# Two transformer-like layers on one core: the shift rows of the second layer's attention as wide products with a mask, the last gate products in four banks, and a new order list

## The reference

```python
Q, K = apply_rope(Q), apply_rope(K)                      # 16 heads of 16
attn = einsum('bqhd,bkhd->bhqk', Q, K) * head_dim ** -0.5
attn = softmax(where(causal, attn, NEG_INF))
out = einsum('bhqk,bkhd->bqhd', attn, V) @ w_proj + b_proj
...
h = silu(tlin(x, w1_w, w1_s)) * tlin(x, w2_w, w2_s)      # 256 -> 1024, the gate products
h = gelu(tlin(h, h1_w, h1_s)); h = gelu(tlin(h, h2_w, h2_s))   # 1024 -> 1024
return tlin(h, w3_w, w3_s)                               # 1024 -> 256
```

## Time and profile before

| what | value |
|---|---|
| median of 3 runs | 1990.87 us (1989.52 to 1991.04) |
| time of the profiled execution | 1990.24 us |
| its span | 1988.5 us |
| PE busy | 1866.2 us, 94% |
| DVE busy | 1359.8 us, 68% |
| ACT busy | 904.1 us, 45% |
| POOL busy | 509.0 us, 26% |
| chain that ended last | PE 74%, DVE 14%, ACT 5%, issue 3% |

### The profile page before, as it was taken

The page is one execution under the profiler, slowest core; times in us unless marked ns, Lnnn a source line. Parts: engine busy times, 40 slices in busy tenths (PEclk is TensorE's granted clock), DMA queues, the critical chain, the costliest instruction groups (busy, mean ns, idle before and its releaser), DMA issues.

```text
span 1988.5 us, 40531 instructions
## 1 busy us (share of the span) xinstructions
PE 1866.2 (94%) x16217; PEld 1308.3 (66%) x16217; DVE 1359.8 (68%) x2382; ACT 904.1 (45%) x1134; POOL 509.0 (26%) x597
## 2 busy tenths in 40 slices
PE   7999999998999997787999999999999999999988
PEld 4665756565656664444677776776776776776767
DVE  5667686767677568778678678587587687686353
ACT  2556555645565654332434524524424434433411
POOL 2435343434444343111211203103103103112020
PEclk8899999999999999898999999999999999999999
DMA  7221212222322000400122231231231321321321
GB/s 191 54 53 43 60 34 62 50 58 50 82 51 63 2 23 1 170 1 16 46 83 73 65 88 48 76 95 30 75 96 33 94 86 51 87 71 57 114 67 43
DMA packets 171818, 126.36 MB, mean 64 GB/s; under 512 B 113944, under 2 KB 148720, under 8 KB 171248
## 3 DMA queue, kind: packets, MB, share of 16 engines
q1 hardware_dynamic: 170800, 123.74, 22.4%
q10 hardware_dynamic: 832, 0.01, 0.0%
HBM read 103.66 MB, written 20.03 MB: 62 GB/s over the span
## 4 chain that ended last, share of the span: by engine, by line
PE 74%; DVE 14%; ACT 5%; issue 3%; SPq 1%; POOL 1%; DMA 1%; DVEq 0%; ACTq 0%; POOLq 0%
PE ps L2028 24%; PE ps L2012 4%; PE ps L1077 4%; PE ps L1908 3%; PE ps L1971 3%; PE ps L982 3%; PE ps L2042 3%; PE ps L1937 3%; DVE b_maxima L1688 3%; PE ps L1951 2%; PE ps L1107 2%; PE ps L1955 2%; PE ps L1040 2%; PE ps L1022 2%; PE ps L1129 2%
## 5 line engine op out<-in xcount | busy, mean ns | idle before, releaser
L2028 PE MATMUL ps<-b_acts,b_hidden_w 128*128 128x512 f32 x2048 | 504.4, 399 | 0.7 <-DVEq L1769 0.7
L2028 PEld LDWEIGHTS ps<-b_acts,b_hidden_w 128*128 128x128 f32 x2048 | 376.3, 188 | 92.1 <-issue 12.9
L452 POOL TENSOR_SCALAR_AFFINE_SELECT a_probs<-a_probs 128x512 f32<-128x512 f32 (+1 forms) x224 | 166.1, 757 | 374.0 <-ACT a_probs L862 249.5
L1607 POOL TENSOR_SCALAR_AFFINE_SELECT b_work<-b_work 128x512 f32<-128x512 f32 x128 | 82.4, 657 | 659.6 <-ACT b_work L1833 659.5
L862 ACT ACTIVATE a_probs<-ps 128x2048 f32<-128x2048 f32 (+1 forms) x96 | 153.1, 1595 | 141.6 <-DVEq L712 104.8
L1865 ACT ACTIVATE b_acts_exact<-ps,c_s 128x512 f32<-128x512 f32 x128 | 88.2, 689 | 273.6 <-PE ps L2028 273.3
L1833 ACT ACTIVATE b_work<-ps 128x2048 f32<-128x2048 f32 (+1 forms) x96 | 153.3, 1596 | 88.5 <-PE ps L1955 87.0
L1688 DVE TENSOR_REDUCE b_maxima<-ps 128x4 f32<-128x2048 f32 (+3 forms) x128 | 187.8, 1488 | 3.3
L1778 DVE CAST b_acts<-b_acts_exact 128x512 fp32r<-128x512 f32 x128 | 60.5, 473 | 166.0 <-ACT b_acts_exact L1865 165.7
L1077 PE MATMUL ps<-a_probs,c_va 128*17 128x192 f32 (+4 forms) x2048 | 134.3, 380 | 4.7 <-issue 2.2
L1685 DVE TENSOR_TENSOR ps<-ps,c_causalr 128x512 f32<-128x512 f32 x128 | 86.1, 695 | 43.3 <-PE ps L1937 41.6
(11 more groups left out here) (242 smaller groups left out, 3611.5 us busy)
## 6 DMA issues: line engine op xcount, KB each, us to landing
b_hidden_w<-turned_h SPq DMA_DIRECT2D x128, 512.0 KB, 3.5
a_raw_next<-in_L_ffn_h_w SPq DMA_DIRECT2D x512, 16.0 KB, 1.8
turned_h<-a_staged SPq DMA_DIRECT2D x32, 256.0 KB, 2.1
a_x<-in_L_attn_x SPq DMA_DIRECT2D x8, 512.0 KB, 4.2
x_mid<-a_x SPq DMA_DIRECT2D x16, 256.0 KB, 2.2
c_x<-x_mid SPq DMA_DIRECT2D x8, 512.0 KB, 4.8
out<-c_x SPq DMA_DIRECT2D x16, 256.0 KB, 2.2
turned_w<-a_staged SPq DMA_DIRECT2D x12, 256.0 KB, 2.6
```

What stands on the lines that cost most here:

```text
L452: return nc.gpsimd.affine_select(out=z, in_=z, compare_op=ALU.is_ge, fill=0.0, base=0, pattern=[[0, blocks_n], [1, cols]], channel_multipl ...
L2028: ins = nc.tensor.matmul(here, view(hidden_w[:, m, k]), view(src[:, k, i]), start=(k + i == 0), stop=(k == NHID - 1 and i == 1))
```

## The change

1. `shift_cols` is a tile of its own, and `again` is one product of 512 columns: `shift_cols` as the stationary side, the identity four times over as the moving side. DVE multiplies it by `shift_rows`, so that each of the four 128-column blocks keeps the rows of its own query tile only. ACT's copy is gone.
2. `att` adds the shift with one set of four products for each key block, of 512, 384, 256 and 128 columns, with a stationary side of ones.
3. POOL's clearing of `shift_cols` no longer waits for the end of the first layer's attention.
4. In the last pass the gate products of odd hidden tiles go to banks 0 and 1, those of even ones to 6 and 7, and the rounding copy is made by ACT instead of DVE.
5. The order list is another one throughout. It has the same entries. The second layer's first entry is now at 711, and most entries have moved by a few places.

```diff
-        self.shift_rows = sb("shift_rows", [P, NT], F32R)
+        self.shift_rows = sb("shift_rows", [P, NT + 1], F32R)
...
+        once(nc.vector.memset(shift_rows[:, NT:NT + 1].bitcast(F32), 1.0))
...
-        return ("f0", "f1")[step[3]]
+        last_pass_odd = step[1] == B - 1 and step[2] % 2
+        return (("g0", "g1") if last_pass_odd else ("f0", "f1"))[step[3]]
...
-    shift = sb("shift", [P, P], F32R)
+    shift = kept.ksplit[:, 3]
+    shift_cols = sb("shift_cols", [P, 4, R])
...
-                first_filled(pool, "lin", QUADS * B - 1, 2)
-                first_filled(pool, "win", QUADS * B - 1, 1)
-                nc.gpsimd.memset(shift_cols, 0.0).then_inc(shift_zero, 1)
+                nc.gpsimd.memset(shift_cols[:], 0.0).then_inc(shift_zero, 1)
...
+            elif name == "again":
+                free = arrive(step)
+                by_tile = room[slot_of(step)].rearrange("p (t q) -> p t q", q=P)
+                nc.vector.tensor_tensor(shift.rearrange("p (t q) -> p t q", q=P), by_tile, shift_rows[:, 0:NT].bitcast(F32).unsqueeze(2).broadcast_to([P, NT, P]),
+                                        ALU.mult).then_inc(free, 1)
...
-                    nc.vector.tensor_copy(act_a[:, i, 0], z).then_inc(a_high, 1)
+                    if b < B - 1:
+                        nc.vector.tensor_copy(act_a[:, i, 0], z).then_inc(a_high, 1)
+                    else:
+                        dve.sem_inc(z_ready, 1)
...
+        def copy_high(i):
+            act.wait_ge(z_ready, i + 1)
+            nc.scalar.copy(act_a[:, i, 0], exact_a[:, i]).then_inc(a_high, 1)
...
-                nc.scalar.copy(shift[:], here[:, 0:P]).then_inc(free, 1)
...
+                if b == B - 1 and i:
+                    copy_high(i - 1)
+            elif step == ("up", B - 1, NHID - 1, 1):
+                copy_high(NHID - 1)
...
-                ins = nc.tensor.transpose(here[:, 0:P], shift_cols.rearrange("p h r -> p (h r)"), ident)
+                ins = nc.tensor.matmul(here.rearrange("p (t q) -> p t q", q=P), shift_cols[:].bitcast(F32R).rearrange("p h r -> p (h r)"),
+                                       identr[:, None, :].broadcast_to([P, NT, P]), start=True, stop=True)
...
-                    for t in range(kb, NT):
-                        at = o + (t - kb) * P
-                        for i in range(4):
-                            nc.tensor.matmul(here[:, i, at:at + P], shift_rows[rows_of(i), t:t + 1].broadcast_to([R, P]), shift[rows_of(i)],
-                                             start=True, stop=False, skip_group_check=True)
+                    for i in range(4):
+                        nc.tensor.matmul(here[:, i, o:o + S - kb * P], shift_rows[rows_of(i), NT:NT + 1].broadcast_to([R, P]), shift[rows_of(i), kb * P:S],
+                                         start=True, stop=False, skip_group_check=True)
```

More of the change, by code:

```diff
@@ L1206 @@
[L1206 to L1209, removed]
@@ new lines @@
+1:proj.1.2 1:proj.1.3 0:r.7.0 0:kk.7.1 1:ga.0 1:tq.1.0 1:out.0.0 1:tk.1.0 1:max.1.0.0 1:tq.1.1 1:max.1.0.1 1:out.0.1 1:tk.1.1 1:max.1.0.2 0:r.7.1
+0:last.7.0 1:xT.0 1:again.1.0 0:last.7.1 1:att.1.0.0 1:split.0 1:max.1.1.0 1:up.0.0.0 1:up.0.0.1 1:values.1.0.0 1:att.1.0.1 1:up.0.1.0 1:up.0.1.1
+1:att.1.0.2 1:max.1.1.1 1:tk.1.2 1:values.1.0.1 1:tq.1.2 1:max.1.1.2 1:up.0.2.0 1:again.1.1 1:max.1.2.0 1:values.1.0.2 1:up.0.2.1 1:up.0.3.0
+1:heads.1.0 1:att.1.1.0 1:up.0.3.1 1:up.0.4.0 1:att.1.1.1 1:up.0.4.1 1:max.1.2.1 1:values.1.1.0 1:up.0.5.0 1:max.1.2.2 1:values.1.1.1 1:up.0.5.1
@@ new lines @@
+1:h2.0.0.0 1:h2.0.0.1 1:h2.0.1.0 1:tq.2.0 1:h2.0.1.1 1:tk.2.0 1:h2.0.2.0 1:max.2.0.0 1:h2.0.2.1 1:tk.2.1 1:h2.0.3.0 1:max.2.0.1 1:h2.0.3.1 1:h2.0.4.0
+1:tq.2.1 1:max.2.0.2 1:h2.0.4.1 1:h2.0.5.0 1:max.2.1.0 1:heads.1.3 1:h2.0.5.1 1:h2.0.6.0 1:max.2.1.1 1:turn.1.1 1:h2.0.6.1 1:h2.0.7.0 1:again.2.0
+1:max.2.1.2 1:ga.1 1:h2.0.7.1 1:out.1.0 1:att.2.0.0 1:last.0.0.0 1:out.1.1 1:att.2.0.1 1:last.0.0.1 1:values.2.0.0 1:att.2.0.2 1:tq.2.2 1:last.0.1.0
+1:xT.1 1:again.2.1 1:split.1 1:values.2.0.1 1:tk.2.2 1:att.2.1.0 1:last.0.1.1 1:up.1.0.0 1:max.2.2.0 1:values.2.0.2 1:up.1.0.1 1:up.1.1.0
@@ new lines @@
+1:tk.4.1 1:h2.2.5.0 1:max.4.1.0 1:h2.2.5.1 1:out.3.0 1:max.4.1.1 1:again.4.0 1:h2.2.6.0 1:h2.2.6.1 1:h2.2.7.0 1:h2.2.7.1 1:att.4.0.0 1:out.3.1
+1:last.2.0.0 1:att.4.0.1 1:last.2.0.1 1:xT.3 1:split.3 1:values.4.0.0 1:values.4.0.1 1:att.4.0.2 1:tk.4.2 1:max.4.1.2 1:values.4.0.2 1:tq.4.2
+1:last.2.1.0 1:again.4.1 1:max.4.2.0 1:last.2.1.1 1:up.3.0.0 1:att.4.1.0 1:heads.4.0 1:up.3.0.1 1:up.3.1.0 1:att.4.1.1 1:up.3.1.1 1:up.3.2.0
+1:max.4.2.1 1:values.4.1.0 1:up.3.2.1 1:values.4.1.1 1:up.3.3.0 1:att.4.1.2 1:max.4.2.2 1:tk.4.3 1:up.3.3.1 1:up.3.4.0 1:values.4.1.2 1:again.4.2
@@ new lines @@
+1:h2.5.6.0 1:max.7.1.1 1:ga.6 1:turn.6.1 1:h2.5.6.1 1:h2.5.7.0 1:again.7.0 1:max.7.1.2 1:out.6.0 1:h2.5.7.1 1:att.7.0.0 1:out.6.1 1:last.5.0.0
+1:att.7.0.1 1:values.7.0.0 1:last.5.0.1 1:xT.6 1:last.5.1.0 1:values.7.0.1 1:split.6 1:att.7.0.2 1:again.7.1 1:last.5.1.1 1:tk.7.2 1:up.6.0.0 1:tq.7.2
+1:att.7.1.0 1:up.6.0.1 1:up.6.1.0 1:max.7.2.0 1:values.7.0.2 1:up.6.1.1 1:up.6.2.0 1:heads.7.0 1:values.7.1.0 1:att.7.1.1 1:up.6.2.1 1:up.6.3.0
+1:att.7.1.2 1:up.6.3.1 1:tk.7.3 1:max.7.2.1 1:up.6.4.0 1:values.7.1.1 1:max.7.2.2 1:up.6.4.1 1:up.6.5.0 1:again.7.2 1:values.7.1.2 1:up.6.5.1
@@ L1329 @@
+1:h2.7.1.1 1:h2.7.2.0 1:h2.7.2.1 1:h2.7.3.0 1:h2.7.3.1 1:h2.7.4.0 1:h2.7.4.1 1:h2.7.5.0 1:h2.7.5.1 1:h2.7.6.0 1:h2.7.6.1 1:h2.7.7.0 1:h2.7.7.1
+1:last.7.0.0 1:last.7.0.1 1:last.7.1.0 1:last.7.1.1
 """
@@ L1822, in run @@
                 nc.scalar.copy(ksplit[:, step[2] % 2], here).then_inc(free, 1)
-            elif name == "again":
-                here, free = arrive(step)
-                nc.scalar.copy(shift[:], here[:, 0:P]).then_inc(free, 1)
             elif name == "att":
```

238 lines of the change are left out of this document (112 added, 126 removed).

## The result

| | median | runs |
|---|---|---|
| before, in the same sessions | 1989.15 us | 1985.69 to 1998.25 (8) |
| changed | 1979.80 us | 1977.21 to 1985.63 (8) |

The ratio is 0.9943, with a 95% interval of [0.9929, 0.9957]: 11 us faster. (The two medians of the table lie 9.4 us apart; differences in us are ratios on 1991 from here on.) The forecast was 1982 us, -8.9.

What follows compares the result with a forecast made beforehand. PE bounds the kernel, busy 916.8 of 930 us from 960 to 1890 us. Shift work -5.9, mask +2, last pass -5.0 sum to -8.9 from 1990.2: 1981.3, predicted 1982 us; eight-in-ten range 1971 to 1994, likeliest case 1976 to 1987.

Steps and rivals of the forecast that it cites:

- The wide sets: Attention's shift products on PE: four wide sets replace ten small ones, saving 0.31 us a group, 9.9 us over 32 groups.
- upper bound, 0.66: Most the wide shift sets could save per group in us, if each of four sets cost 0.11 or, first in a fill, 0.16.
- The turning product: PE's product turning the shift maxima, 512 columns instead of a 128-column transpose: 0.13 us more a group, 4.0 us in all.
- The two together: Wide shift sets and the longer turning product on PE: 9.9 saved less 4.0 added, 5.9 us less work.
- The last pass: Last pass's gate products: other banks and rounding off DVE let PE run through, 5.0 us gained (4.1 to 5.5).
- The mask on DVE: Shift multiplication moved from ACT's 0.27 us copy to DVE's 0.70: nothing from 960 us on, 2 us before.
- the join: Six groups up to 960 us, where DVE's shift multiplication can show: 2 us taken, 2.6 if 0.43 each, at most 6.8.
- price without cover: Cost of DVE's shift multiplication if list entries did not hide it: 0.43 us a group, 13.8 us over 32.
- the rival's condition: Each group's `att` waits for DVE's shift multiplication: 13.8 us in place of 2, total 1994, chance 0.12.
- The order: Whole new order list: taken as nothing, between 12 us gained and 18 lost; chances 0.15 gain, 0.11 loss.
- The sum: All terms for the whole kernel: -5.9 + 2 - 5.0 = -8.9 us, giving 1981.3, predicted as 1982 us.
- What would have shown it wrong: PE idle before the second layer's feed-forward changing by over 6 us, or `att.0` waiting for DVE in most groups.

Runs made afterwards that it cites:

- order_only: The kernel before with the new order list and no other edit; +3.2 us, ratio 1.0016 against the kernel before.
- last_pass_only: The kernel before, old list, with only the last pass's four banks and rounding on ACT; -4.6 us, ratio 0.9977 against the kernel before.
- shift_only: The kernel before, old list, with only the shift edits (512-column product, DVE mask, wide sets, POOL's clearing); +36 us, ratio 1.0179 against the kernel before.
- old_order: The changed kernel's code with the old order list; +28.5 us, ratio 1.0143 against the kernel before.
- act_mask_old_order: The changed kernel with the old list and the mask made by ACT in four copies; -7.4 us, ratio 0.9963 against the kernel before.
- spliced: The changed kernel with the new list for its first 902 entries and the old one behind; +12.3 us, ratio 1.0062 against the kernel before.
- copy_on_dve: The kernel before with the copy of the 128 turned shift columns made by DVE instead of ACT; +42 us, ratio 1.0211 against the kernel before.
- banks_alone: The changed kernel with the last pass's rounding copy on DVE again; 1979.73 us, ratio 0.9943 against the kernel before.

## Why the total was right and two of its prices were not

**The wide sets: the step's own number right, the term too small.** The blocks of shift products take 0.89 us a group for 0.90. But "time that a block of shift products takes is the distance from its start to that of the scores behind it" left out what the block does to the scores. The medians over 32 groups, start to start:

```
us         shift block   first scores   second scores, to what follows
512 before    0.498         0.283            0.334
512 after     0.334         0.232            0.329
384 before    0.388         0.225            0.175
384 after     0.277         0.174            0.176
256 before    0.276         0.168            0.218
256 after     0.221         0.118            0.220
128 before    0.059         0.111            0.213
128 after     0.057         0.112            0.214
```

The change from narrow to wide sets costs 0.05 us each time, and stood in the scores' account before. A wide set behind a wide one takes 0.232, 0.174 and 0.118 us, not half of a pair (0.31, 0.20, 0.19). So the group saves 0.485 us, not 0.31, and 32 groups 15.5, not 9.9. The rule of the Trainium skill that I weighed in the forecast ("TensorE: Matmul & The Clock Gate", section "Wait — 56ns, not 53.3ns?") gave 0.21 us for 512 columns, 0.10 for a small set and 0.42 saved; I set it aside because "the 0.31 us of a wide one does not" agree. The trace agrees with it to about a tenth once the switch and the hand-over are taken off (0.232 and 0.111), and it was nearer than my reading. (The forecast's upper bound, 0.66, does not follow from its own terms: 3 x 0.16 + 0.11 = 0.59 leaves 0.62. Nothing hangs on it.)

**The turning product: right.** From its start to the next instruction 0.34 us, 0.20 before: 0.14 for 0.13, 4.4 us for 4.0.

**The two together** are then -11.1 us and not -5.9, by the medians of the starts. 27 of the 32 groups lie in the stretch, -9.3. PE's busy time there (its length less its idle time) is 954.6 us in `order_only` and 946.9 in the changed kernel, -7.7. That agrees but does not measure it, as executions with the same instructions of PE in the stretch differ by up to 8 us: with the old code and the old list it is 950.2 and 947.7 us (`before`, `last_pass_only`), with the new code and the old list 945.6, 949.7 and 941.4 (`shift_only`, `old_order`, `act_mask_old_order`), with the new code and list 946.7 to 950.6 in four kernels. So in the old list this number shows no clear saving. Some of the work behind long waits runs at half clock there, as the copy's did above; how much was not separated.

**The last pass: right, with a term left out.** I took 5.0 (4.1 to 5.5). The gate products became 7.1 us shorter, more than the bank waits, and 1.3 were given back behind them: 5.8, and 4.6 by the runs of `last_pass_only`. Four products take 0.907 us from start to start there, not 1.03 as amid the attention, so that a tile takes PE 1.81 us. Then my sentence "all are under PE's, so PE runs through" holds for the gate products and fails behind them: DVE's two multiplications take 0.69 + 0.75 us, and 0.32 and 0.16 pass between them (one waits for the result of the one before), 1.91 us a tile. DVE falls behind by 0.1 us a tile, its last multiplication starts at 1905.96, 1.5 us after PE's last gate product, and the remainder comes at 1908.85, 4.4 us after the first hidden product and not the 2.9 of the forecast.

**The mask on DVE: the price was wrong, the outcome right.** For this list "so I take nothing there" holds: 1.0 us of waits of `att.0` in 32 groups, 0.4 of the next user's weight loads. At the join I took +2; against `order_only` it became 0.4 us shorter. What failed is the price without cover. I gave 0.43 us a group, the difference of two lengths, 13.8 us in all, and 0.70 + 0.43 at most at the join. In the old list the shift edits cost 36 us together, though they take work from PE, and a copy that is not longer at all costs 42. The step confused how long the instruction is with how long its result takes: in the old list DVE's start comes 1.3 us later than ACT's on average, and is 3.8 and 4.8 us behind the product in the two groups shown. Nor is a late start a price by itself: in the changed kernel one mask starts 5.4 us after its product, and PE waits for nothing, since `att.0` stands far enough behind. Had the rival's condition come true, its 1994 would have been the 2020 of `old_order`. The queue rule of the Trainium skill ("TensorE: Matmul & The Clock Gate", section "Architectural detail: the array is 16× 32×32, not 1× 128×128"), told against the edit, named that wait, but I priced it by the mask's own length. Also, I weighed the distance from `again` to `att.0` only. About a third of the waits in `shift_only` (12.5 of 34.6 us) are those of the next user of `misc`.

**The order: "for the whole list I take nothing" is right by accident.** Old code: +3.2. New code: -40. Its value has no number apart from the code that it serves: by the distances, the entries between `again` and `att.0` rose from 2.5 to 3.5, which I did read, and that is probably what it is for. The 5.1 us less in the first layer of the profiled execution: the six kernels with the old list lie at 782 to 791 there, `order_only` and `spliced`, which have the new one, at 786, and the other five with it at 777 to 781. The means are 781 with the new list and 786 with the old one, so the list may well bring it, but the spread is as large as the effect and it is not shown.

**The sum.** In parts, against the kernel before: order with the old code +3.2, last pass -4.6 to -5.8, and the rest, -9 to -10, the shift edits under the new list (which were not run by themselves), where I had -5.9 + 2 = -3.9. The blocks' own -11.1 with 1 to 2 us for the mask would give that; this last is argued from what is left, not measured. So the total agrees to 2.5 us by the ratio because one term that was 5 us too small met 3 us of the order that were taken as nothing: right in sign and place, and partly by luck in size.

**What would have shown it wrong.** PE's idle time ahead of the second layer's first gate product went from 90.2 to 90.9 us, and its waits for the mask from 960 on are 0.3 us, both as foretold. From 960 to 1890 us PE's idle time is 15.7 us, not 13, and its work 2.5 us less, not 5, though these windows hold other work in another list. The last gate products took 15.5 us, not 17 to 18.

Not tried was turning the shift columns in four separate blocks, which would need neither the mask nor the turning product of 512 columns, as the first layer does.

## What to carry to other kernels

Moving a short operation to another engine cost the place in that engine's queue first here and its length second: read from the trace how long after its input the new engine would start it, group by group, and whom the result or the freed bank serves next, all of them. A hand-written order and the code that it was made for are one thing; time both codes under both orders before either is given a value. The price of an instruction that shares an engine with its neighbours is the distance between the same two neighbours before and after, not the distance to the next one alone. When a wait for banks is taken from the fastest engine, work out the cycle of the others with the idle time between their own dependent instructions, not only with their lengths.

## What the runs showed of the hardware

- Sets of four products of 32 rows, side by side: 0.232, 0.174, 0.118 and 0.112 us for 512, 384, 256 and 128 columns from start to start behind a set of the same width; 0.10 more for the first wide set of a fill, 0.05 for the first narrow one, and 0.05 for a wide set behind a narrow one.
- ACT's copy of 128 columns from PSUM takes 266 ns, with a scale for each partition 368. The Trainium skill ("ScalarE: Activation LUTs", section "What ACT_TABLE_LOAD costs") has about 93 ns for such an operand; here the difference is 102, with the instruction changed from CAST to ACTIVATE as well, so the trace agrees to a tenth.
- DVE leaves 0.16 us between two multiplications of which the second reads the first's result, and 0.32 before the next tile's, where the increment of `z_ready` stands between. In `banks_alone` the copy stands there: it starts 0.15 us after the second multiplication's end, and the next tile's first one before the copy has ended.
- In `copy_on_dve`, after 3.3 us of standing still at 869.1 us, PE went on at a granted clock of 0.50, its 1.2 GHz level, and sixteen small products took 0.89 us in place of 0.50.
